# Block-FP4 feed-forward on Trainium2: rounding step in PSUM, rounding one step sooner, residual behind the products, attention's head in the first drain

## The reference, cut

```
def fp4_linear(x, w):                 # blocks of 16 along the last dim
    return einsum('bsk,nk->bsn', fp4_quant_dequant(x), fp4_quant_dequant(w))
# scale = max|block|/6; round block/scale to 0,.5,1,1.5,2,3,4,6; times scale
def ffn(x):
    h = silu(fp4_linear(x, w_gate)) * fp4_linear(x, w_up)     # 128 -> 352
    return fp4_linear(h, w_down)                               # 352 -> 128
x = x + mamba(layernorm(x));  x = x + ffn(layernorm(x))
x = x + attention(layernorm(x));  x = x + ffn(layernorm(x))
```

## Time and profile before

| what | us |
| --- | --- |
| median of 3 executions (lowest, highest) | 1033.62 (1032.73, 1034.75) |
| the profiled execution, its own time | 1035.28 |
| its span, first to last instruction | 1033.6 |
| mean granted TensorE clock over the span | 0.969 |
| busy: TensorE / VectorE / ScalarE / GpSimd | 949.8 / 902.6 / 761.5 / 760.9 |

### The profile page before, as it was taken

The page is one execution under the profiler, slowest core; times in us unless marked ns, Lnnn a source line. Parts: engine busy times, 40 slices in busy tenths (PEclk is TensorE's granted clock), DMA queues, the critical chain, the costliest instruction groups (busy, mean ns, idle before and its releaser), DMA issues. The chain is left out here.

```text
span 1033.6 us, 29750 instructions
## 1 busy us (share of the span) xinstructions
PE 949.8 (92%) x11909; PEld 580.2 (56%) x11909; DVE 902.6 (87%) x1724; ACT 761.5 (74%) x1683; POOL 760.9 (74%) x426
## 2 busy tenths in 40 slices
PE   5799999999999999999999999988477999999786
PEld 2455555565555555555555555655346566666456
DVE  6879998999989999899998999999699767787597
ACT  5888898988989889899898897984434255555442
POOL 1688999989999899999999989998254223333243
PEclk9799999999999999999999999999888999999888
DMA  6745453544535444454444544440571010000001
GB/s 187 254 160 166 137 173 125 166 147 162 167 128 164 147 165 146 145 167 146 165 146 138 158 147 159 147 132 14 128 155 21 21 23 17 7 2 2 1 0 41
DMA packets 69272, 120.88 MB, mean 117 GB/s; under 512 B 40072, under 2 KB 51152, under 8 KB 60112
## 3 DMA queue, kind: packets, MB, share of 16 engines
q1 hardware_dynamic: 69136, 118.98, 37.3%
HBM read 111.10 MB, written 6.29 MB: 114 GB/s over the span
## 5 line engine op out<-in xcount | busy, mean ns | idle before, releaser
L902 DVE TENSOR_TENSOR_SCAN hid<-decay,acc 128x256 f32<-128x256 f32 x1024 | 604.6, 664 | 40.9 <-PE acc L539 40.4
L1002 POOL TENSOR_TENSOR prod<-hid,c_rep 128x1024 f32<-128x1024 f32 x256 | 600.7, 2380 | 43.8 <-DVE hid L902 32.9
L765 ACT ACTIVATE decay<-delta,a_neg 128x255 f32<-128x255 f32 x1024 | 428.4, 502 | 47.6 <-DVE hid L902 47.4
L539 PE MATMUL acc<-b_diag,du_t 64*64 64x256 f32 x4096 | 273.1, 383 | 15.9 <-DVE hid L902 12.2
L567 PE MATMUL ring<-prod,ident 64*64 64x256 f32 x4096 | 255.5, 379 | 2.2 <-POOL prod L1002 2.2
L539 PEld LDWEIGHTS acc<-b_diag,du_t 64*64 64x64 f32 x4096 | 147.9, 134 | 124.8 <-DVE hid L902 55.3
L567 PEld LDWEIGHTS ring<-prod,ident 64*64 64x64 f32 x4096 | 152.0, 133 | 83.5 <-issue 22.7
L1916 POOL TENSOR_SCALAR_AFFINE_SELECT att_probs<-att_probs 128x512 f32<-128x512 f32 x64 | 41.1, 642 | 102.5 <-ACT att_probs L1959 100.1
L1959 ACT ACTIVATE att_probs<-acc 128x384 f32<-128x384 f32 x128 | 55.8, 488 | 52.5 <-PE acc L1733 52.5
L444 PE MATMUL ring<-xpad,diag_cw 64*64 64x512 f32 x512 | 60.5, 589 | 0.0
L1116 POOL TENSOR_TENSOR ffn_h_value<-ffn_h,ffn_h_inv 128x704 f32<-128x704 f32 x16 | 23.7, 1480 | 43.2 <-DVE ffn_h_value L1139 32.5
(11 more groups left out here) (180 smaller groups left out, 1263.7 us busy)
## 6 DMA issues: line engine op xcount, KB each, us to landing
c_rep<-c_rows SPq DMA_DIRECT2D x64, 1024.0 KB, 4.7
b_diag<-diag_rows SPq DMA_DIRECT2D x62, 512.0 KB, 3.9
diag_rows<-zeros SPq DMA_DIRECT2D x2, 2048.0 KB, 12.4
att_qk<-in_pos_q SPq DMA_DIRECT2D x4, 768.0 KB
att_qk<-in_pos_k SPq DMA_DIRECT2D x4, 768.0 KB
att_qk<-att_dense SPq DMA_DIRECT2D x24, 64.0 KB
resid<-in_x SPq DMA_DIRECT2D x4, 256.0 KB, 3.9
c_rows<-bc SPq DMA_DIRECT2D x64, 8.0 KB, 1.5
```

The lines of the kernel that those rows point to most:

```text
L539: last = nc.tensor.matmul(inj[m * HALF:(m + 1) * HALF, K % 2, at:at + HALF * SG], du_t[rows, n % 2, e, chans:chans + HALF], b_diag[rows, K ...
L765: last = nc.scalar.activation(decay[:, K % DECAYS, s, 1:], delta[:, n % 2, h, e * SEQ + 1:(e + 1) * SEQ], ACT.Exp, scale=a_neg[:, lay(n) % ...
L902: last = nc.vector.tensor_tensor_scan(hid[:, K % HIDS, s, :], decay[:, K % DECAYS, s, :], rows[:, s, :], 0.0, ALU.mult, ALU.add)
L1002: nc.gpsimd.tensor_tensor(prod[:, K // 2 % PRODS, h], hid[:, K % HIDS, :, :], c_rep[:, g, :, at], ALU.mult).then_inc(s_prod, 1)
```

## The change

- `Rounder` takes a tile `held` for the finished rounding step. For h it is PSUM, `acc` 2 and 3 (704 columns across the bank border); there is one, so `scalar_step(k)` waits for the rounding of k-1. For x, value and result now lie in `core.normed` itself (`value_tile`, `xq` gone).
- The rounding of step k-1 stands in round k, not k-2, behind the scales of step k; its exponent heads round k. GpSimd's round k is dequant k-2 (behind a wait for the exponent of k-1), then normal k. TensorE's is `turn_h(k-2)`, `down(k-3)`. The loops are one round shorter.
- The gate banks stay two. Turned h lies in ring 0 and half of acc 1, and `down` has one result, the other half of acc 1. So `down(k)` waits for add k-1 and for the copy of the third part of turned h of step k+1, and `turn_h(k)` for add k-2. The third part is turned and copied first.
- The residual add of step k-4 stands inside `hidden(k)`, behind the two products.
- Attention's moments of chunk 0 come before `hidden(7)`, its normalise behind it; all four strips, the first values and the GpSimd fills move into `ffn1`'s block; q0 and q1 swap banks.
- `ffn2` no longer starts with ScalarE's copy of turned x, but with the last chunk's rstd and the Silu table load; that chunk's normalise comes behind the second copy, its scales in round 1.

```diff
-    def __init__(self, core, sb, tag, blocks, depth=2):
-        self.core, self.blocks, self.depth = core, blocks, depth
+    def __init__(self, core, sb, tag, blocks, depth=2, held=None, values=None):
+        self.core, self.blocks, self.depth, self.held = core, blocks, depth, held
...
-        self.value = sb(f"{tag}_value", [P, depth, blocks * BLK])
+        self.values = values or [self.value_tile(sb, tag, n) for n in range(depth)]
...
+    def steps(self, i):
+
+        return self.step[:, i, :] if self.held is None else self.held
 
     def scalar_step(self, a, c):
         i = c % self.depth
         a.wait_ge(self.s_exponent, c + 1)
-        self.core.nc.scalar.activation(self.step[:, i, :], self.step[:, i, :], ACT.Relu, bias=self.core.minus_step[:, :],
+        if self.held is not None and c:
+            self.s_round.wait(a, "rounded", c - 1)
+        self.core.nc.scalar.activation(self.steps(i), self.step[:, i, :], ACT.Relu, bias=self.core.minus_step[:, :],
                                        scale=HALF_STEP).then_inc(self.s_step, 1)
 
...
-        gate_bank = [bank(ring, 1), bank(ring, 2)]
-        up_bank = [bank(ring, 3), bank(acc, 0)]
-        hT_bank = [bank(acc, 1)[:, 0:2 * P], bank(acc, 1)[:, 2 * P:4 * P], bank(acc, 2)[:, 0:2 * P]]
-        down_bank = [bank(acc, 3)[:, 0:2 * P], bank(ring, 0)[:, 0:2 * P]]
+        qh = Rounder(core, sb, "h", HCOLS // BLK, 4, acc[:, 2 * BANK:2 * BANK + HCOLS])
+        x_bank, gate_bank, up_bank = bank(ring, 0), [bank(ring, 1), bank(ring, 2)], [bank(ring, 3), bank(acc, 0)]
+        hT_bank = [bank(ring, 0)[:, 0:2 * P], bank(ring, 0)[:, 2 * P:4 * P], bank(acc, 1)[:, 0:2 * P]]
+        down_bank = bank(acc, 1)[:, 2 * P:4 * P]
...
+                    if k >= 4:
+                        add(k - 4)
                     v.wait_ge(s_h, 2 * (k + 1))
                     qh.vector_scales(v, qh.blocked(h[:, k % 2, :]), k)
 
                 def add(k):
                     v.wait_ge(s_down, k + 1)
                     at = resid_flat[:, k * 2 * P:(k + 1) * 2 * P]
-                    nc.vector.tensor_tensor(at, at, down_bank[k % 2], ALU.add).then_inc(s_add, 1)
...
-                for k in range(HSTEPS + 3):
+                for k in range(HSTEPS + 1):
+                    if k >= 2:
+                        qh.vector_exponent(v, k - 1)
+                    if k == 2:
+                        x.q.vector_exponent(v, 3)
+                    if attention and k == HSTEPS - 1:
+                        v.wait_ge(s_add, 2)
+                        attention.norm.vector_moments(v, 0)
                     if k < HSTEPS:
                         hidden(k)
-                    if k == 1 and not early:
+                    if k == HSTEPS:
+                        add(k - 4)
+                    if attention and k == HSTEPS - 1:
+                        attention.norm.vector_normalise(v, 0)
+                    if k == 0 and early == 0:
+                        x.q.vector_exponent(v, 2)
+                    if k == 1:
+                        qh.vector_exponent(v, 0)
                         x.vector_scales(v, 3)
-                    if 1 <= k <= HSTEPS:
-                        qh.vector_exponent(v, k - 1)
-                    if k in (0, 2) and k // 2 + 2 >= early:
-                        x.q.vector_exponent(v, k // 2 + 2)
-                    if 2 <= k <= HSTEPS + 1:
-                        qh.vector_round(v, k - 2)
-                    if k in (1, 3) and k // 2 + 2 >= early:
-                        x.q.vector_round(v, k // 2 + 2)
-                    if attention and k == HSTEPS + 2:
-                        attention.norm.vector_normalise(v, 0)
-                    if k >= 5:
-                        add(k - 5)
-                    if attention and k == HSTEPS + 1:
-                        v.wait_ge(s_add, 2)
-                        attention.norm.vector_moments(v, 0)
+                    if k >= 1:
+                        qh.vector_round(v, k - 1)
+                    if k == 1 and early == 0:
+                        x.q.vector_round(v, 2)
+                    if k == 2:
+                        x.q.vector_round(v, 3)
                 if attention:
                     v.wait_ge(s_add, 4)
                     attention.norm.vector_moments(v, 1)
-                for k in range(HSTEPS - 2, HSTEPS):
+                for k in range(HSTEPS - 3, HSTEPS):
                     add(k)
                 if attention:
+                    attention.wait(v)
+                    attention.vector_strips(v, 0)
                     attention.norm.vector_normalise(v, 1)
-                    attention.wait(v)
-                    for g in range(2):
+                    for g in range(1, HGROUPS):
                         attention.vector_strips(v, g)
+                    attention.vector_values(v, 0)
...
-                for k in range(1, HSTEPS + 3):
-                    if 3 <= k < HSTEPS:
-                        qh.s_round.wait(p, "rounded", k - 3)
-                    if k <= HSTEPS:
-                        h_normal(k - 1)
-                    if k >= 3:
-                        h_dequant(k - 3)
-                    if k in (2, 4) and k // 2 + 1 >= early:
-                        x.pool_dequant(p, k // 2 + 1)
-                    if k == 2 and not early:
+                for k in range(HSTEPS + 2):
+                    if k >= 2:
+                        p.wait_ge(qh.s_exponent, min(k, HSTEPS))
+                        h_dequant(k - 2)
+                    if k < HSTEPS:
+                        h_normal(k)
+                    if k == 1:
                         x.pool_normal(p, 3)
+                    if k == 1 and early == 0:
+                        x.pool_dequant(p, 2)
+                    if k == 2:
+                        x.pool_dequant(p, 3)
+                if attention:
+                    attention.pool_set(p)
...
+                    need(t, s_add, k - 1)
+                    t.wait_ge(s_xTc, 3 if k < 2 else 4)
+                    for j in (2, 0, 1):
+                        for i in range(2):
+                            at = i * FFN + j * P
+                            last = nc.tensor.transpose(hT_bank[j][0:FK[j], i * P:(i + 1) * P], hq[:, k % 2, at:at + FK[j]], ident[:, :])
+                        if j == 2:
+                            last.then_inc(s_hT2, 1)
+                    last.then_inc(s_hT, 1)
+
+                def down(k):
+                    t.wait_ge(s_hTc, k + 1)
+                    need(t, s_hT2c, min(k + 2, HSTEPS))
+                    need(t, s_add, k)
                     for i in range(2):
                         for j in range(FTILES):
-                            at = i * FFN + j * P
-                            last = nc.tensor.transpose(hT_bank[j][0:FK[j], i * P:(i + 1) * P], hq[:, k % 2, at:at + FK[j]], ident[:, :])
-                    last.then_inc(s_hT, 1)
-
-                def down(k):
-                    t.wait_ge(s_hTc, k + 1)
-                    need(t, s_add, k - 1)
-                    if k == 1:
-                        t.wait_ge(s_xTc, CHUNKS)
-                    for i in range(2):
-                        for j in range(FTILES):
-                            last = nc.tensor.matmul(down_bank[k % 2][:, i * P:(i + 1) * P], hqT[0:FK[j], k % 2, j, i * P:(i + 1) * P],
+                            last = nc.tensor.matmul(down_bank[:, i * P:(i + 1) * P], hqT[0:FK[j], k % 2, j, i * P:(i + 1) * P],
                                                     core.wdT[0:FK[j], j, :], start=(j == 0), stop=(j == FTILES - 1))
                     last.then_inc(s_down, 1)
 
                 turn_x(0)
                 gate_up(0)
                 turn_x(1)
-                for k in range(HSTEPS + 3):
+                for k in range(HSTEPS + 2):
                     if k + 1 < HSTEPS:
                         gate_up(k + 1)
                     if k in (2, 4):
                         turn_x(k // 2 + 1)
+                    if k >= 2:
+                        turn_h(k - 2)
                     if k >= 3:
-                        turn_h(k - 3)
-                    if k >= 4:
-                        down(k - 4)
-                if attention:
-                    t.wait_ge(s_h, 2 * HSTEPS)
-                    attention.tensor_turn(t)
+                        down(k - 3)
+                    if attention and k == HSTEPS - 1:
+                        t.wait_ge(s_h, 2 * HSTEPS)
+                        attention.tensor_turn(t)
                 down(HSTEPS - 1)
                 if attention:
                     attention.wait(t)
-                    t.wait_ge(s_silu, 2 * HSTEPS)
-                    t.wait_ge(s_xTc, CHUNKS)
+                    t.wait_ge(s_hTc, HSTEPS)
+                    qh.s_round.wait(t, "rounded", HSTEPS - 1)
                     attention.tensor_strips(t, 0)
+                    attention.tensor_strips(t, 1)
                     t.wait_ge(s_add, HSTEPS)
-                    attention.tensor_strips(t, 1)
```

(36 more changed lines are left out.)

147 lines of the change are left out of this document (77 added, 70 removed).

## The result

The changed kernel takes **1042.05 us** (median of 6, 1039.69 to 1057.55), the kernel before 1034.76 (1032.73 to 1035.15). The ratio is 1.0062, 95% interval 1.0046 to 1.0077. I had said 1030.7, range 1026.4 to 1034.4, so the change made the kernel slower where I had forecast faster, and the time lies outside the range. (Medians here are over all runs and ratios leave disturbed ones out; where the two disagree, as for the two entry experiments and the step in SBUF, the ratio counts.)

What follows compares the result with a forecast made beforehand. VectorE was taken to bound the feed-forwards, with a second loss in the chain ending each stage. Gains of 0.5 (`ffn1`), 0.2 (attention's head) and 2.2 (`ffn2`) made 2.9, from 1033.62 to 1030.7 us, range 1026.4 to 1034.4.

Steps and rivals of the forecast that it cites:

- Part 1: Middle of the feed-forwards: one step takes VectorE 5.06 us instead of 5.69.
- Hold gone: Middle of the feed-forwards: VectorE's L1106 no longer waits behind GpSimd's dequant, 0.51 us less a step.
- 0.065 us for a source in PSUM: Rounding with its step in PSUM: by the skill 2.1 us more over 32 operations; the forecast charged nothing.
- ScalarE writing PSUM: Rounding step of h written to PSUM: taken as 0.88 us, bound 0.2 us in all over the two ends.
- Part 2: `ffn1`: `down(7)` ends at 801.5 instead of 801.97, gain 0.5 us, bounds 3.2 and -1.2.
- so I take part of it at 1.2 GHz: +1.3, bounds 0 and 3.0: End of `ffn1`, reused for `ffn2`: TensorE partly at the low clock lengthens the last chain by 1.3 us.
- the held L1056: Round 7 of `ffn1`: attention's normalise, 1.0 us, starts with GpSimd's normal and is held 1.4 us.
- the chain at full clock: Ends of both feed-forwards: 9.4 us from exponent through `down(7)`, and 0.4 for the last add.
- Part 3: Attention's head, from `down(7)` to the first score reduction: 10.8 instead of 11.0 us, gain 0.2, bounds 1.0 and -0.5.
- Part 4: `ffn2`: start loses 1.85 us, yet the last add comes at 1029.0 instead of 1031.24; gain 2.2, bounds 3.6 and -0.5.
- (b): Both ends at 1.2 GHz throughout, 3.0 instead of 1.3 each, or rounding pays for PSUM: about 1033.4 us; chance 0.27.
- (c): Middle of the feed-forwards: TensorE becomes the bound at low clock, up to 3 us a step, 1036.7 us; chance 0.07.

Runs made afterwards that it cites:

- the two entry experiments: Changed kernel with `ffn2`'s first copy of turned x ahead of the rstd and Silu table load again, run twice: ratios 1.0026 and 1.0024.
- the step in SBUF: Changed kernel with the one held rounding step of h in SBUF instead of PSUM: 1056.83 us, ratio 1.0192.
- the idle products: Products nobody reads, filling TensorE's waits: seven in the changed kernel's ends, 1037.18 us; nine and five in the ends of the kernel before, 1035.06 us.
- The kernel before, filled in ends and first halves: Kernel before with unread products: fourteen in each end, nine in the first half of `ffn1`, seven in that of `ffn2`: 1036.72 us, ratio 1.0005.
- own banks alone: Changed kernel with the results of the last three `down` products in banks of their own: 1038.64 us median, ratio 1.0008.
- nine: Changed kernel with seven unread products in its ends and one each before attention's turn of x and the last turn of h: 1039.27 us.
- all edits: Changed kernel with own banks, seven unread products, `down(6)` ahead of `turn_h(7)`, and `ffn2`'s copy ahead of the table load: 1030.36 us.
- the two best versions: Changed kernel with all edits, 1030.36 us; and the same with unread products in the feed-forward first halves too, 1027.51 us.

## Why the prediction was wrong

**Part 1 held.** Hold gone, 5.04 us a round against 5.06, VectorE indifferent to PSUM. The 0.065 us for a source in PSUM, my estimate from the Trainium skill's figures ("VectorE: DVE Perf Modes", section on the TRN2 errata), isn't seen here: L1155 takes 0.88 with its step in PSUM and 0.88 unheld in SBUF. ScalarE writing PSUM took 0.85, against 0.88. One round of each stage, 771.00 to 776.73 in `ffn1`, took 5.73, with an add waiting 0.59 for its product.

**Part 2 failed at its last step, "so I take part of it at 1.2 GHz: +1.3, bounds 0 and 3.0".** The exponent was right, the held L1056 too (2.18, for 1.11 unheld). The term measured 4.4 (10.4 with the clock at 1.00, 14.8 with it at 0.5), outside its bounds, in both stages. Three faults. I counted two products on the chain; with one result tile there are three, `down(5)` too, because `turn_h(7)` waits for add 5, which I had written and not priced. Then I took under half of my own bound, as the earlier trace rows has 0.73 and not 0.5 (the end of `ffn2` before, 1018 to 1031.3, has 0.74); after the change all three ran at 0.50. And the chain at full clock was 0.6 short, 10.4 for 9.8 with the add. Together 3.7 us per end, 7.5 of the 8.6. The path was another, too: I priced the way to `turn_h(7)` through its own dequant, which ends at 794.89; it started at 796.91, behind `down(5)` and add 5. At full clock, with the idle products, the two come within 0.2 us of each other (794.75 and 794.96), which is why my path gave nearly the right length for 2.4 GHz only.

**The comparison hid it.** Before, the end of `ffn1` is bounded by VectorE: from the last exponent on, that exponent (held, 1.66 for 0.52), two roundings (one held), with adds and moments between.

```profile
789.80 1.66 DVE L1124 TENSOR_SCALAR ffn_h_step<-ffn_h_value 128x704 uint32<-128x704 uint32 x1
...
793.44 2.03 DVE L1137 SCALAR_TENSOR_TENSOR ffn_h_value<-ffn_h_step,ffn_h_value 128x704 f32<-128x704 f32 x1
```

So a slow TensorE is free there; the idle products show it, 12.63 either way. The change empties VectorE's queue and leaves a chain of TensorE and adds. The low clock that cost nothing costs 4.4 us after it. I took over the clock of before without asking who had been waiting for TensorE then, and who would now.

**Part 3**: -0.2 forecast, +0.35 measured in the table; the 0.35 is the first half of the strips begun at a low clock (3.94 for eight products, 3.60 at full clock). At full clock the stretch takes 10.60 to 10.64 in the runs with idle products in the end, before it took 10.54: the gain of 0.2 isn't there. Undone in the changed kernel the move costs 2.2 us in that stretch, 1.7 of them clock, and 1.2 in the median, whose ranges overlap. **Part 4**: the entry lost 2.05 against my 1.85 (second h product 8.72 us behind the moments, before 6.67), with the copy behind the table load:

```profile
973.53 1.28 ACT L1478 ACT_TABLE_LOAD   x1
974.83 0.60 ACT L1458 ACTIVATE ffn_xqT<-ring 128x512 f32<-128x512 f32 x1
```

The rest of it is Part 2's fault over again. Attention's +1.24 was in no part: its last 11 us have a mean granted clock of 0.70, before 0.91. The kernel before, filled in ends and first halves, goes with it: 0.71 there, and attention 155.95. Why the clock is lower there stays open.

**The rivals**: (b) named the mechanism, a series at 1.2 GHz throughout, and got 0.27, but priced it with my bound of 3.0, hence "no change". (c) had TensorE as the bound in the middle. That was small in the changed kernel, the one round of 5.73 in each stage, but real with seven idle products, 2.0 us in two rounds of `ffn2`. None of the rivals priced a slow end above 3.0, so the range couldn't hold the result.

**Open**: why attention starts at 1.2 GHz with own banks alone (0.51 over 811 to 824), with seven idle products (0.62 over 811 to 820), with nine (0.57) and with the step in SBUF (0.59 over 818 to 824), but not before, not after, and not with all edits. Filled gaps don't explain it, nor does "an end at full clock hands it on", since the kernel before with full ends and the two best versions show none. It isn't fixed by the program either: with own banks alone the time went from 1030.56 at a mean granted clock of 0.968 to 1048.23 at 0.951. It wasn't tried further.

## What to carry to other kernels

Price the clock on the chain that is critical after the change, not on the one before: list every product in the line from last input to last result, and take all of them at 1.2 GHz as one bound. Here three times 1.27 alone, 3.8, is above my 3.0. If a buffer is saved by going from two result tiles to one, look where the pipeline drains: in the middle of the kernel before it cost 0.2 us at most, in the drain of the changed one 1.5 us at full clock, and 3.9 where its waits also kept the clock low. And where TensorE idles in a drain, a few products into a free bank are the cheapest experiment there is: they tell in one run what the clock costs in that stretch. Read the stretch and not the kernel's time, since the low clock can turn up elsewhere: alone they made 1042 into 1037 us, with own banks and the old entry 1030, and used in the first halves too, 1027.5.
